# Four spectral products summed by accumulating stores from GpSimd's queue, and an inverse transform that loads the sums

## The chip, the cores and the metric

The kernel runs on one core of a Trainium2 chip. The metric is device time in microseconds (us) of one execution. A core has five engines with instruction streams of their own: PE (TensorE, matrix products), ACT (ScalarE), DVE (VectorE), POOL (GpSimd) and SP (SyncE, used here only to issue transfers). They meet through semaphores. Transfers (DMAs) run on 16 DMA engines that all queues share.

## The reference

Input x is (4, 56, 56, 128). Layer 0 is a neighbourhood-attention block (7x7 windows, 4 heads) with an MLP. Layer 1 works on the tokens t (4, 3136, 128): a linear attention that is added to t, and then the part that the change is in, a spectral filter (STU):

```python
def _stu_conv(phi, u, n):                      # n = 8192
    Vf = jnp.fft.rfft(phi, n=n, axis=0)        # 16 filters
    Uf_p = jnp.fft.rfft(u, n=n, axis=1)
    Uf_m = jnp.fft.rfft(u * sgn3, n=n, axis=1)
    U_plus  = jnp.fft.irfft(Vf[None, :, :, None] * Uf_p[:, :, None, :], n=n, axis=1)[:, :sl]
    U_minus = jnp.fft.irfft(Vf[None, :, :, None] * Uf_m[:, :, None, :], n=n, axis=1)[:, :sl]
    return U_plus, U_minus * sgn[None, :, None, None]
out = einsum('btkd,k,kde->bte', U_plus, s, Mpp) + einsum('btkd,k,kde->bte', U_minus, s, Mpm)
out = out + sum_i  shift(u, i) @ Mu[i]         # three taps
# four such sums over the first T/1, T/2, T/4, T/8 tokens, weighted by a straight-through gumbel choice
```

For each frequency the spectrum of the tokens (complex) is multiplied by a filter spectrum that has already absorbed the matrices (complex). One complex product needs four real ones: real = RR - II, imaginary = RI + IR.

## The kernel before, in words

The work runs in four parts. Front (0 to about 830 us) is layer 0, the linear attention and the preparation of the filter; Spectrum (about 735 to 875 us, beside the end of the front) is the forward transform of the tokens, stored to HBM as Ud. Neither is touched except for layout, names of semaphores and one constant.

Filters (875 to 1646 us) goes through 784 frequency slots in 28 chunks of 28 slots. `Filters.STAGES` is 56. A group P of four stages (4P to 4P+3) works on chunks 2P and 2P+1, and half the output features at a time: after stages 4P and 4P+1 the sums of the first 64 features are whole (store 2P), after stages 4P+2 and 4P+3 those of the others (store 2P+1). All engines follow one list of steps, written out in `order()` (L1326 to L1346), each in its own program order. Per stage there are 32 `filter` steps (PE makes a spectrum of the filter in a PSUM bank, L1374 and L1377; ACT copies the even ones to SBUF, L1415, and DVE the odd ones, L1429) and 28 `sums` steps (PE multiplies it with the tokens' spectrum, L1396). Filter products use four banks in turn, so product u waits until product u-4 has been copied (L1366, L1367); a `whole` one (i % 8 < 4) is issued as a pair and waits for two copies. In stage order, sums 7 to 13 follow filters 8 to 15 of the next stage, and then comes filter 16. The sums of an odd stage leave PSUM for the tile YS (L1421, ACT, after sums 7, 15, 23 and 27). SP stores YS to Yd in four transfers (L1493), all four real products of every frequency. In ACT's program the copy of YS after sums 7 stands ahead of its copies of filters 12 and 14.

GpSimd's program before holds only the `load` steps: `planes` (L1446 to L1474) rotates chunk c into one of three buffers U7. Chunk c takes the buffer of chunk c-3, so it waits (L1439) until PE has done the sums on that: chunk 2P+3 waits for half the sums of stage 4P+3 (14 of 28), chunk 2P+4 for all of them. In the list, `load 2P+3` stands at the head of stage 4P, `store 2P` behind stage 4P+1, `load 2P+4` at the head of stage 4P+3 and `store 2P+1` behind stage 4P+3. SP's `load` waits until the tile UL is free, which is when `planes` of the chunk before has ended (L1298).

Inverse (1646 to 1844 us) loads Yd (`load_y`, L1522), forms the two differences and sums on DVE (`combine`, L1648 to L1670, result YC), and PE does the inverse transform (L1596), 24 products for each of 16 steps t, plus a reversal (`turn`, L1603). DVE adds the parts into RN, which SP stores to the output.

Of the kernel before, what the change touches and what calls it, by code (L numbers as in the profile page):

```python
# [11 lines left out]
G = 98  # L12
# [222 lines left out]
class Front:  # L235
# [235 lines left out]
    def scalar(self, e):  # L471
        S, col = self.S, self.col
        for k, n in self.order:
# [21 lines left out]
            elif k == "q_keep":  # L495
# [10 lines left out]
                if i == 0 and b < 2:  # L506
                    e.wait_ge(S["kzero"], b + 1)
# [332 lines left out]
    def gpsimd(self, q):  # L840
        S, ch = self.S, self.pool_steps
        for k, n in self.order:
            if k == "setup" and n == 0:
# [8 lines left out]
                q.memset(self.kP[0][:, :, :], 0.0).then_inc(S["kzero"], 1)  # L852
# [5 lines left out]
            elif k == "setup" and n == 2:  # L858
                q.memset(self.kP[1][:, :, :], 0.0).then_inc(S["kzero"], 1)
# [20 lines left out]
            elif k == "z_clear":  # L880
                zero = self.kP[1].rearrange("p a b -> p (a b)")
                if n == 0:
                    q.wait_ge(S["kzero"], 2)
# [4 lines left out]
            elif k == "a_ones":  # L888
                q.wait_ge(S["csum"], NJ * n + NJ)
                if n:  # L890
                    q.wait_ge(S["kvmm"], n)
                q.tensor_scalar(self.kv[:, 1, :], self.ones, self.cs[n % 2][:, 128:129], None, ALU.mult).then_inc(S["kv1"], 1)
            elif k == "a_pre":
                q.wait_ge(S["xnc"], 2 * n + 2)
                q.wait_ge(S["kvw"], 2 * (n // NJ) + 2)
                q.tensor_tensor(self.rows(n), self.rows(n), self.kv[0:TB, 4:5, :].broadcast_to([TB, 4, 128]),
                                ALU.add).then_inc(S["addkv"], 1)
            elif k == "p_load":
                q.memset(self.sg, 1.0).then_inc(S["pset"], 1)
                for par in range(2):  # L900
                    q.dma_start(self.D["VbD"][par, :, KF:KT], self.D["c_ar"][par]).then_inc(S["d_ar"], 16)
# [28 lines left out]
    def setup(self, e, part):  # L930
# [15 lines left out]
        e.dma_start(self.ident[:, :], D["c_id"]).then_inc(S["d_first"], 16)  # L946
# [25 lines left out]
    def sync(self, e):  # L972
        S, D = self.S, self.D
        for k, n in self.order:
# [39 lines left out]
            elif k == "p_load":  # L1014
# [3 lines left out]
                e.wait_ge(S["pset"], 1)  # L1018
# [289 lines left out]
class Filters:  # L1308
# [44 lines left out]
    def tensor(self, e):  # L1353
        S = self.S
        for k, s, i in self.order():
# [24 lines left out]
            elif k == "sums":  # L1380
# [10 lines left out]
                if par == 0 and i % 8 == 0 and s >= 2:  # L1391
                    e.wait_ge(S["ys"], 4 * (s // 2 - 1) + bk + 1)
# [17 lines left out]
    def scalar(self, e):  # L1410
        S = self.S
        for k, s, i in self.order():
# [3 lines left out]
            elif k == "sums" and s % 2 and i in (7, 15, 23, 27):  # L1416
                bk, n = i // 8, 2 if i == 27 else 4
                e.wait_ge(S["sums"], 28 * s + i + 1)
                if s >= 2:
                    e.wait_ge(S["d_y"], 64 * (s // 2))  # L1420
                e.activation(self.YS[:, 4 * bk:4 * bk + n, :].rearrange("p g x -> p (g x)"),  # L1421
                             self.banks[:, 2048 + 512 * bk:2048 + 512 * bk + 128 * n], ACT.Copy).then_inc(S["ys"], 1)

    def vector(self, v):
        S = self.S
        for k, s, i in self.order():
            if k == "filter" and i % 2:
                dst, src = self.evict_filter(v, s, i)
                v.tensor_copy(dst, src).then_inc(S["gm_dve"], 1)  # L1429

    def gpsimd(self, q):
# [14 lines left out]
    def planes(self, q, c, u, u7, w, n):  # L1446

        S, ch = self.S, self.pool_steps
        a = u7.rearrange("d s (m r b) -> d s m r b", m=7, r=2)[:, :, 0:3]
# [3 lines left out]
        same, got = u7[:, :, 24:56].rearrange("d s (x b) -> d s x b", b=4), u.rearrange("d b s x -> d s x b")  # L1453
        if c < NCH // 2:
            q.tensor_copy(same, got)  # L1455
        else:
            src = same.rearrange("d s (m r) b -> d s m r b", r=2)
            q.tensor_tensor(same[:, 0:n:2], got[:, 0:n:2], got[:, 1:n:2], ALU.add)  # L1458
            ch.tick(q.tensor_tensor(same[:, 1:n:2], got[:, 0:n:2], got[:, 1:n:2], ALU.subtract))
            q.wait_ge(ch.sem, ch.n)  # L1460
            if c == NCH // 2:
                q.tensor_copy(same[:, 0], got[:, 0])
                ch.tick(q.tensor_scalar(same[:, 1], got[:, 1], -1.0, None, ALU.mult))
                q.wait_ge(ch.sem, ch.n)
# [10 lines left out]

    def sync(self, e):
        S, D = self.S, self.D
        for k, c, _ in self.order():
# [10 lines left out]
            elif k == "store":  # L1489
                e.wait_ge(S["ys"], 4 * c + 4)  # L1490
                P, half = c // 2, c % 2
                for x in range(4):
                    e.dma_start(D["Yd"][56 * P:56 * P + 56].rearrange("(g s) r h x -> s r g h x", s=4)[x, :, :, half, :],  # L1493
                                self.YS[32 * x:32 * x + 32, :, :]).then_inc(S["d_y"], 16)
            elif k == "inverse":
# [3 lines left out]
                elif c == 2:  # L1499
                    e.wait_ge(S["d_y"], 64 * (NCH // 2))  # L1500
                    for a in range(4):
                        load_y(e, D, D["YL0"], a, 0, 0).then_inc(S["d_ylh"], 16)
                else:
                    e.wait_ge(S["d_y"], 64 * (NCH - 2))
# [46 lines left out]
class Inverse:  # L1551
# [4 lines left out]
    def __init__(self, nc, ctx, D, S, chains):  # L1556
# [3 lines left out]
        yl1 = sb("YL1", [G, 8192])  # L1560
        D["YL1"] = [yl1[:, 0:4096], yl1[:, 4096:8192]]
        self.YL = [D["YL0"], D["YL1"]]
        self.YC = [sb("YC0", [G, 2, 8, 2, 128])]
        D["rev"] = sb("rev2", [G, G])[:, :]
        self.YC.append(sb("YC1", [G, 2, 8, 2, 128]))
# [20 lines left out]
    def sums(self, e, kind, t, a0, a1):  # L1586
# [19 lines left out]
    def tensor(self, e):  # L1606
        S = self.S
        e.wait_ge(S["d_iv"], 32)
        e.wait_ge(S["yc"], 1)
# [3 lines left out]
        e.wait_ge(S["yc"], 2)  # L1613
        e.wait_ge(S["ys"], 4 * NCH)
# [3 lines left out]
        e.wait_ge(S["yc"], 3)  # L1618
# [5 lines left out]
        for t in range(2, 16):  # L1624
            if t % 2 == 0:
                e.wait_ge(S["yc"], t + 2)
# [5 lines left out]
            if t % 2 == 0:  # L1632
                e.wait_ge(S["yc"], t + 3)
# [14 lines left out]
    def combine(self, v, n, h, k, a0=0, a1=4):  # L1648

        S = self.S  # L1650
        yl = self.YL[n % 2][h].rearrange("p (n r h k e) -> p n r h k e", n=8, r=2, h=2, k=2)[:, 2 * a0:2 * a1]
        yc = self.YC[n % 2].rearrange("p k a q (h e) -> p k (a q) h e", h=2)
        if k == 0 and a0 == 0:
            if n == 0:
                v.wait_ge(S["d_ylh" if h == 0 else "d_yl0"], 64 if h == 0 else 48)
                v.wait_ge(S["sums"], 28 * (Filters.STAGES - 1))
            elif h == 0:
                v.wait_ge(S[f"d_yl{n % 2}"], (48 if n % 2 == 0 else 128) + 128 * (n // 2))
                if n >= 2:
                    v.wait_ge(S["idft"], 8 * (n - 1))  # L1660
        if a0 == 3 and k == 0:
            v.wait_ge(S["d_ylh"], 80)
        hs, op = slice(8 * h + 2 * a0, 8 * h + 2 * a1), (ALU.subtract, ALU.add)[k]
        ins = v.tensor_tensor(yc[:, k, hs], yl[:, :, 0, :, k], yl[:, :, 1, :, 1 - k], op)
        if h == 0:
            self.steps.tick(ins)
            v.wait_ge(self.steps.sem, self.steps.n)
            ins = v.tensor_copy(yc[0:1, k, 0:2], yl[0:1, 0:2, k, :, k])  # L1668
        if k == 1:
            ins.then_inc(S["yc"], 1)  # L1670

    def vector(self, v):
        S, w, ch = self.S, self.D["wsel"], self.steps
        for k in range(2):
            self.combine(v, 0, 0, k)
        for k in range(2):
            self.combine(v, 0, 1, k, 0, 3)
        for k in range(2):
            self.combine(v, 0, 1, k, 3, 4)
        for t in range(17):  # L1680
# [15 lines left out]
            if t < 16:  # L1696
                rn = self.RN[n % 2]
                if q == 0 and 0 < n < 7:
                    for k in range(2):
                        self.combine(v, n + 1, 1, k)  # L1700
# [16 lines left out]
                if t == 0:  # L1717
                    for h in range(2):
                        for k in range(2):
                            self.combine(v, 1, h, k)  # L1720
                if q == 1 and n + 2 < 8:
                    for k in range(2):
                        self.combine(v, n + 2, 0, k)

    def sync(self, e):
        S, D = self.S, self.D
        for n in range(8):
            if n + 2 < 8:
                e.wait_ge(S["yc"], 2 * n + 3)
                for a in range(8):  # L1730
                    load_y(e, D, self.YL[n % 2], a, (n + 2) // 2, n % 2).then_inc(S[f"d_yl{n % 2}"], 16)
# [14 lines left out]
INVERSE_SIGNALS = "yc idft half gh rows tdif tmm turned kept d_rn0 d_rn1 d_o0 d_o1".split()  # L1746


def program(nc, x, ln1_w, ln1_b, w_qkv, b_qkv, rpb, w_proj, b_proj, ln2_w, ln2_b, w_fc1, b_fc1, w_fc2, b_fc2,
            Wq, bq, Wk, bk, Wv, bv, sigma, phi, M_u, M_pp, M_pm, log_w, gumbel,  # L1750
            c_id, c_fwd, c_vdft, c_tw, c_inv, c_ar, c_msk, c_rev, out):
    with ExitStack() as ctx:
# [12 lines left out]
                 Un=dr("Un", [NB, SLOTS, 512]), Ud=dr("Ud", [128, NB, SLOTS * 8]), Yd=dr("Yd", [SLOTS, 32, 2, 128]),  # L1765
# [4 lines left out]
                 YL0=[zone[0:G, 4096:8192], zone[0:G, 12288:16384]], banks=banks)  # L1770
# [31 lines left out]
def tables():  # L1802
# [42 lines left out]
    C2[392:, 196:] *= -1.0  # L1845
    inv = np.stack([C1, C2], 0).reshape(2, 8, 98, 392).transpose(2, 0, 1, 3)
# [4 lines left out]
def shape_constants():  # L1851
# [8 lines left out]
    return {"c_id": np.eye(128, dtype=np.float32), "c_fwd": fwd, "c_vdft": vdft, "c_tw": tw, "c_inv": inv,  # L1860
# [23 lines left out]
```

## Time and profile before

| | us |
|---|---|
| median of 3 runs (1840.15 to 1850.67) | 1843.27 |
| the profiled execution | 1845.46 |
| its span (first to last instruction) | 1844.1 |
| PE busy in the span | 1735.1 (94%) |
| DVE busy | 1314.0 (71%) |
| ACT busy | 1200.3 (65%) |
| POOL busy | 638.5 (35%) |

The profile covers one execution. A "busy" engine runs an instruction. A wait is put down to the instruction that came last. PEclk is the granted clock of TensorE as a share of full speed. The DMA share is that of the 16 DMA engines together. A queue named SPq or POOLq is the issuing side of a transfer; "to landing" is from the issue until the data are there.

### The profile page before, as it was taken

What the parts mean: (1) busy time and instruction counts of PE and PEld (TensorE: products, weight loads), DVE (VectorE), ACT (ScalarE), POOL (GpSimd) and SP (SyncE); (2) the same over time, 40 slices, a digit from 0 to 9 for tenths busy, and PEclk for the clock granted to TensorE, in tenths of its full rate; (3) what the DMA queues carried; (4) which work ended last, traced back from release to release, by engine and by line L of the source; (5) the groups of instructions that cost most, each with busy time, mean ns of one, the idle gap of its engine ahead of it and who ended that gap; (6) DMA issues with size and microseconds to landing.
All of it is one profiled execution on the core that took longest, in us unless ns stands there. A gap on an engine that the chain in (4) does not pass through costs nothing.

```text
span 1844.1 us, 76476 instructions
## 1 busy us (share of the span) xinstructions
PE 1735.1 (94%) x32475; PEld 1391.2 (75%) x32475; DVE 1314.0 (71%) x3787; ACT 1200.3 (65%) x2619; POOL 638.5 (35%) x815
## 2 busy tenths in 40 slices
PE   5899999999999998988899999999999999999998
PEld 3566666666767666888788888888888888876666
DVE  2677778888877766694677777777777777647666
ACT  5788888887877654556677777777777777640000
POOL 6555555655555533040533122333323233100000
PEclk8999999999999998989999999999999999999999
DMA  4422333433233313387322212222221222368772
GB/s 118 114 80 75 104 84 91 113 90 97 73 99 85 95 53 98 132 242 231 94 56 59 56 46 68 68 59 57 58 58 45 68 68 55 89 177 215 209 203 78
DMA packets 266001, 182.52 MB, mean 99 GB/s; under 512 B 39888, under 2 KB 263022, under 8 KB 263966
## 3 DMA queue, kind: packets, MB, share of 16 engines
q1 hardware_dynamic: 262782, 176.07, 35.2%
q8 instruction: 258, 4.23, 0.9%
q0 software_dynamic: 640, 1.16, 0.2%
q10 hardware_dynamic: 2240, 0.40, 0.1%
q14 instruction: 81, 0.66, 0.1%
HBM read 107.03 MB, written 70.63 MB: 96 GB/s over the span
## 4 chain that ended last, share of the span: by engine, by line
PE 66%; DVE 13%; issue 5%; DMA 5%; POOL 4%; ACT 4%; SPq 3%; DVEq 0%; POOLq 0%; ACTq 0%
PE banks L1396 20%; PE banks L1374 10%; PE banks L1377 9%; PE banks L406 5%; DVE zone L607 4%; PE banks L400 3%; PE banks L1596 3%; PE banks L365 2%; SPq L1524 2%; PE banks L355 2%; DMA YL<-Yd 2%; PE banks L413 2%; PE banks L379 2%; DVE st L594 1%; PE banks L453 1%
## 5 line engine op out<-in xcount | busy, mean ns | idle before, releaser
L1429 DVE COPY Gm<-banks 128x448 f32<-128x448 f32 x896 | 553.2, 639 | 214.2 <-PE banks L1374 127.4
L1415 ACT ACTIVATE Gm<-banks 128x448 f32<-128x448 f32 x896 | 515.6, 629 | 202.7 <-PE banks L1374 151.3
L1396 PE MATMUL banks<-Gm,U 128*32 128x128 f32 x12544 | 519.0, 275 | 15.0 <-issue 8.7
L1396 PEld LDWEIGHTS banks<-Gm,U 128*32 128x32 f32 x12544 | 340.4, 110 | 60.2 <-issue 54.7
L1377 PE MATMUL banks<-V,zone 118*32 118x224 bf16 x7040 | 294.3, 260 | 0.5 <-issue 0.4
L1374 PE MATMUL banks<-V,zone 118*128 118x224 bf16 x1824 | 215.3, 261 | 0.8 <-ACT qT L1203 0.5
L869 POOL TENSOR_TENSOR W<-W,mx 128x280 f32<-128x280 f32 x196 | 130.6, 666 | 227.4 <-DVE mx L656 226.0
L1377 PEld LDWEIGHTS banks<-V,zone 118*32 118x32 bf16 x7040 | 194.9, 96 | 1.8 <-issue 1.4
L1374 PEld LDWEIGHTS banks<-V,zone 118*128 118x128 bf16 x1824 | 157.1, 98 | 47.3 <-issue 39.2
L1596 PE MATMUL banks<-YC,zone 98*98 98x256 f32 x768 | 171.3, 383 | 3.3 <-DVE YC L1668 3.3
L1596 PEld LDWEIGHTS banks<-YC,zone 98*98 98x98 f32 x768 | 128.1, 167 | 50.3 <-issue 7.6
L519 ACT ACTIVATE W<-W,mx 128x140 f32<-128x140 f32 x392 | 156.7, 404 | 0.3
L607 DVE TENSOR_SCALAR zone<-XR,zone 112x128 f32<-112x128 f32 x336 | 152.1, 498 | 4.6 <-POOL zone L831 3.2
L365 PE MATMUL banks<-ident,W 128*98 128x128 f32 x784 | 123.3, 281 | 24.4 <-ACT W L529 15.2
L649 DVE CUSTOM_DVE_ANT_0 W<-banks,zone 128x140 f32<-128x140 f32 x392 | 102.6, 298 | 54.3 <-PE banks L355 27.0
L365 PEld LDWEIGHTS banks<-ident,W 128*98 128x98 f32 x784 | 87.0, 130 | 62.9 <-POOL W L869 36.5
L529 ACT ACTIVATE W<-banks 98x512 f32<-98x512 f32 x196 | 115.1, 587 | 28.4 <-PE banks L365 27.8
L831 POOL TENSOR_TENSOR zone<-zone 112x4 f32<-112x4 f32 x112 | 119.6, 1068 | 9.3
L1646 ACT ACTIVATE PB<-banks 98x512 f32<-98x512 f32 x16 | 9.6, 598 | 173.1 <-PE banks L1596 173.1
L1455 POOL COPY U<-UL 128x896 f32<-128x896 f32 (+2 forms) x14 | 24.2, 1730 | 276.6 <-PE banks L1396 205.8
L594 DVE BATCH_NORM_STATS2 st<-XR 112x6 f32<-112x128 f32 x448 | 107.4, 281 | 8.4 <-DMA XR<-in_x_dram 5.8
L1458 POOL TENSOR_TENSOR U<-UL 128x448 f32<-128x448 f32 x14 | 25.3, 1805 | 252.9 <-PE banks L1396 232.1
(174 smaller groups left out, 2684.8 us busy)
## 6 DMA issues: line engine op xcount, KB each, us to landing
Yd<-YS SPq DMA_DIRECT2D x112, 224.0 KB, 4.3
W<-Vd SPq DMA_DIRECT2D x392, 49.0 KB
zone<-Yd SPq DMA_DIRECT2D x32, 392.0 KB
YL<-Yd SPq DMA_DIRECT2D x32, 392.0 KB
UL<-Ud SPq DMA_DIRECT2D x27, 448.0 KB, 4.0
zone<-Mbf SPq DMA_DIRECT2D x28, 256.0 KB
Vd<-W SPq DMA_DIRECT2D x56, 112.0 KB
T<-XR SPq DMA_DIRECT2D x28, 224.0 KB, 2.6
```

What stands on the lines that cost most here:

```text
L365: ins = e.transpose(self.psum[4][0:G, 256 * c + 128 * j:256 * c + 128 * j + 128], self.PN[n % 3][:, j, G * c:G * c + G], self.ident[:, :])
L519: ins = e.activation(self.PB[n % 3][:, j, :], self.SB[n % 3][:, j, :], ACT.Exp, bias=self.mx[n % 4][:, j:j + 1], scale=-1.0, accum_out=sel ...
L594: ins = v.bn_stats(self.st[:, m, :], self.row(g)[:, 128 * m:128 * m + 128])
L607: ins = v.tensor_scalar(x[:, m, 0:128], self.row(g)[:, 128 * m:128 * m + 128], self.mv[k][g % 2][:, m, 0:1], self.rs[k][g % 2][:, m:m + 1] ...
L831: ins = q.tensor_tensor(rs, rs, self.half[0:TB, :], ALU.pow)
L869: q.tensor_tensor(self.inner(self.PN[n % 3]), self.PB[n % 3], r, ALU.mult).then_inc(S["pn"], 1)
L1374: ins = e.matmul(pt[:, q, :], M, V, start=True, stop=True)
L1377: ins = e.matmul(pt[32 * x:32 * x + 32, q, :], M[:, 32 * x:32 * x + 32], V, start=True, stop=True, tile_position=(0, 32 * x))
L1396: ins = e.matmul(p[32 * x:32 * x + 32, :], self.U7[(2 * P + ch) % 3][:, sl, 8 * (3 - q):8 * (3 - q) + 32], self.Gm[:, par, r:r + 2, :], st ...
L1415: e.activation(dst, src, ACT.Copy).then_inc(S["gm_act"], 1)
L1429: v.tensor_copy(dst, src).then_inc(S["gm_dve"], 1)
L1596: ins = e.matmul(p[:, 256 * c:256 * c + 256], self.D["IV"][c][:, a, x:x + G], self.YC[n % 2][:, int(k), a], start=a == lo and (c == 0 or n ...
```

## The change

- The columns of U7 are ordered so that each group of two neighbouring rows of the sums is the product with the real part (even partition) and the imaginary part (odd partition) of the tokens' spectrum.
- YS is evicted by ACT after sums 7 and 23 and by DVE after sums 15 and 27, each in two instructions; the second multiplies the columns of the filter's imaginary part by +1 on even and -1 on odd partitions. These evictions wait (from stage 3 on) for d_ya, the accumulating transfers of the chunks before, where they waited for the stores d_y.
- A store is one transfer of the 64 even partitions (two transfers and two small ones for the first two chunks). Then GpSimd adds the odd partitions to the same rows with two accumulating transfers (`accum_op=ALU.add`, real and imaginary columns crossed). Its new step `add_up` is taken at the place of `store` in the list.
- Yd holds half as much, `load_y` moves half, three tiles YL are in turn, PE reads them without `combine`, which is gone. The loads for group n=2 are issued ahead of the first `load_out`.
- The constant of the first row of the inverse table changes sign, and some semaphores are merged.

The core of the diff:

```diff
+            elif k == "sums" and s % 2 and i in (7, 23):
+                dst, src = self.evict_sums(e, s, i)
+                e.activation(dst[:, :, 0:64], src[:, :, 0:64], ACT.Copy)
+                e.activation(dst[:, :, 64:128], src[:, :, 64:128], ACT.Copy, scale=self.D["wsel"][:, 16:17]).then_inc(S["ys_act"], 1)
+    def evict_sums(self, e, s, i):
+        S, bk, n = self.S, i // 8, 2 if i == 27 else 4
+        e.wait_ge(S["sums"], 28 * s + i + 1)
+        if s >= 2:
+            e.wait_ge(S["d_ya"], added(s // 2))
 ...
     def gpsimd(self, q):
         S, D = self.S, self.D
         for k, c, _ in self.order():
+            if k == "store":
+                self.add_up(q, c)
             if k != "load":
                 continue
 ...
+    def product_rows(self, c):
+        P, half = c // 2, c % 2
+        rows = self.D["Yd"][896 * P:896 * P + 896, half].rearrange("(g i) x -> i g x", i=64)
+        return [(rows[16:64], 32, 128, 0), (rows[0:16, 1:14], 0, 32, 1)] if P == 0 else [(rows, 0, 128, 0)]
+    def add_up(self, q, c):
+        S = self.S
+        q.wait_ge(S["d_y"], stored(c + 1))
+        for rows, p0, p1, g0 in self.product_rows(c):
+            for k in range(2):
+                q.dma_start(rows[:, :, 64 - 64 * k:128 - 64 * k], self.YS[p0 + 1:p1:2, g0:14, 64 * k:64 * k + 64],
+                            accum_op=ALU.add).then_inc(S["d_ya"], 16)
 ...
             elif k == "store":
-                e.wait_ge(S["ys"], 4 * c + 4)
-                for x in range(4):
-                    e.dma_start(D["Yd"][56 * P:56 * P + 56].rearrange("(g s) r h x -> s r g h x", s=4)[x, :, :, half, :],
-                                self.YS[32 * x:32 * x + 32, :, :]).then_inc(S["d_y"], 16)
+                e.wait_ge(S["ys_act"], 2 * c + 2)
+                e.wait_ge(S["ys_dve"], 2 * c + 2)
+                for rows, p0, p1, g0 in self.product_rows(c):
+                    e.dma_start(rows, self.YS[p0:p1:2, g0:14]).then_inc(S["d_y"], 16)
 ...
         e.wait_ge(S["d_ylh"], 64)
-        e.wait_ge(S["d_y"], 64 * NCH)
+        e.wait_ge(S["d_ya"], added(NCH))
         load_y(e, D, D["YL0"], 7, 0, 0).then_inc(S["d_ylh"], 16)
         load_y(e, D, D["YL1"], 7, 0, 1).then_inc(S["d_yl1"], 16)
         e.wait_ge(S["sums"], 28 * Filters.STAGES)
+        for a in range(8):
+            load_y(e, D, D["YL2"], a, 1, 0).then_inc(S["d_yl2"], 16)
         load_out(e, D, S, 0)
```

## Rows read from the trace of the kernel before

**Rows 1.** Windows (us; busy PE, PEld, DVE, ACT, POOL; PEclk; DMA share; GB/s), Filters.

```profile
1000.00:1100.00 100.00, 99.24 (x2863) 87.22 (x2864) 73.40 (x120) 73.34 (x133) 23.56 (x22) 1.00 0.26 63
```

**Rows 2.** Waits in Filters, 890 to 1645 us: total, times, longest.

```profile
POOL U L1458 <- PE banks L1396: 232.1, 9, 33.1
POOL U L1455 <- PE banks L1396: 205.8, 7, 34.7
```

**Rows 3.** Timeline of POOL (start, us, ...): first and last instruction of `planes`, chunks 3, 4, 17.

```profile
938.88 1.86 POOL L1455 COPY U<-UL 128x896 f32<-128x896 f32 x1 [32.40 <-PE banks L1396]
945.65 1.09 POOL L1474 TENSOR_TENSOR U<-U,UL 128x336 f32<-128x336 f32 x1
950.70 1.86 POOL L1455 COPY U<-UL 128x896 f32<-128x896 f32 x1 [3.95 <-DMA UL<-Ud]
...
1314.55 1.84 POOL L1458 TENSOR_TENSOR U<-UL 128x448 f32<-128x448 f32 x1 [31.86 <-PE banks L1396]
1322.38 1.10 POOL L1474 TENSOR_TENSOR U<-U,UL 128x336 f32<-128x336 f32 x1
```

**Rows 4.** Timeline of ACT: evictions of YS in stage 3 and the first of stage 5.

```profile
936.71 0.60 ACT L1421 ACTIVATE YS<-banks 128x512 f32<-128x512 f32 x1
...
945.43 0.38 ACT L1421 ACTIVATE YS<-banks 128x256 f32<-128x256 f32 x1
963.81 0.60 ACT L1421 ACTIVATE YS<-banks 128x512 f32<-128x512 f32 x1
```

**Rows 5.** Timeline, all engines, about filter 16 of the list in stage 3.

```profile
937.20 1.11 ACT L1415 ACTIVATE Gm<-banks 128x448 f32<-128x448 f32 x2
937.89 0.84 PE L1396 MATMUL banks<-Gm,U 128*32 128x128 f32 x24
938.66 0.94 PE L1374 MATMUL banks<-V,zone 118*128 118x224 bf16 x8
```

**Rows 6.** Groups by line: total busy, mean ns of one.

```profile
L1415 ACT ACTIVATE Gm<-banks 128x448 f32<-128x448 f32 x896 | 515.6, 629 | 202.7 <-PE banks L1374 151.3 <-PE banks L1377 49.4 <-DMA Ud<-qT 1.7
L1462 POOL COPY U<-UL 128x32 f32<-128x32 f32 x1 | 0.2, 233 | 0.1
```

**Rows 7.** GpSimd's transfers of before: durations (ns, min/median/max) of L919; KB each, us to landing.

```profile
L919 POOL DMA_DIRECT2D Vd<-kP x6: 533/548/778, 39.1 to 52.8; - x6
Vd<-kP POOLq DMA_DIRECT2D x6, 93.0 KB, 2.9
```

**Rows 8.** Stores of YS by SP: KB each, us to landing, and windows around the first.

```profile
Yd<-YS SPq DMA_DIRECT2D x112, 224.0 KB, 4.3
918.00:922.00 4.00, 4.00 (x110) 3.44 (x111) 2.96 (x5) 2.97 (x7) 0.00 (x0) 1.00 0.60 138
922.00:926.00 4.00, 4.00 (x132) 3.62 (x128) 3.13 (x6) 2.75 (x6) 0.00 (x0) 1.00 0.53 110
```

**Rows 9.** PE's timeline around an idle stretch of the Spectrum part, and two windows.

```profile
787.01 2.82 PE L1188 MATMUL banks<-XR,W 98*128 98x196 f32 x16
813.58 5.60 PE L1182 MATMUL banks<-XR 98*128 98x196 f32 x16 [6.14 <-DVE XR L1242]
816.00:820.00 4.00, 4.00 (x13) 3.69 (x13) 3.93 (x13) 1.68 (x2) 1.26 (x2) 0.51 1.07 414
820.00:824.00 4.00, 4.00 (x25) 3.75 (x24) 3.83 (x16) 0.97 (x2) 1.26 (x2) 1.00 0.60 179
```

**Rows 10.** Timeline at the start of Inverse: last eviction, store, load of the last piece, PE.

```profile
1645.88 20.96 PE L1596 MATMUL banks<-YC,zone 98*98 98x256 f32 x96
1646.45 5.84 SPq L1493 DMA_DIRECT2D Yd<-YS  x4
1660.49 0.76 DVE L1664 TENSOR_TENSOR YC<-zone 98x256 f32<-98x256 f32 x2 [14.81 <-DMA zone<-Yd]
1671.04 6.45 PE L1596 MATMUL banks<-YC,zone 98*98 98x256 f32 x16 [3.26 <-DVE YC L1668]
```

**Rows 11.** Waits of PE in Inverse, 1645 to 1844 us.

```profile
PE banks L1603 <- DVE DF L1708: 7.3, 6, 1.7
```

More of the change, by code:

```diff
@@ L1415, in scalar @@
                 e.activation(dst, src, ACT.Copy).then_inc(S["gm_act"], 1)
[L1416 to L1422, printed above, removed]
+            elif k == "sums" and s % 2 and i in (7, 23):
[7 more added lines that the diff above has]
+            e.wait_ge(S["d_ya"], added(s // 2))
+        src = self.banks[:, 2048 + 512 * bk:2048 + 512 * bk + 128 * n].rearrange("p (g x) -> p g x", x=128)
+        return self.YS[:, 4 * bk:4 * bk + n], src
     def vector(self, v):
         S = self.S
+        v.wait_ge(S["d_sign"], 16)
         for k, s, i in self.order():
@@ L1429, in vector @@
                 v.tensor_copy(dst, src).then_inc(S["gm_dve"], 1)
+            elif k == "sums" and s % 2 and i in (15, 27):
+                dst, src = self.evict_sums(v, s, i)
+                v.tensor_copy(dst[:, :, 0:64], src[:, :, 0:64])
+                v.tensor_scalar(dst[:, :, 64:128], src[:, :, 64:128], self.D["wsel"][:, 16:17], None, ALU.mult
+                                ).then_inc(S["ys_dve"], 1)
     def gpsimd(self, q):
@@ L1448, in planes @@
         S, ch = self.S, self.pool_steps
-        a = u7.rearrange("d s (m r b) -> d s m r b", m=7, r=2)[:, :, 0:3]
+        a, x7 = (u7.rearrange("d s (m b r) -> d s m r b", m=7, r=2)[:, :, i:j] for i, j in ((0, 3), (3, 7)))
         s4 = u.rearrange("d b s (m r) -> d s m r b", m=4, r=2)
@@ L1452, in planes @@
         src, spare = s4, s4[:, :, 1:4, 0]
[L1453 to L1459, printed above, removed]
-            q.wait_ge(ch.sem, ch.n)
[L1461 to L1464, printed above, removed]
+        for r in range(2):
+            to, of = x7[:, :, :, r], s4[:, :, :, r]
+            if c < NCH // 2:
+                q.tensor_copy(to, of)
+            else:
+                src = x7
+                q.tensor_tensor(to[:, 0:n:2], of[:, 0:n:2], of[:, 1:n:2], ALU.add)
+                ch.tick(q.tensor_tensor(to[:, 1:n:2], of[:, 0:n:2], of[:, 1:n:2], ALU.subtract))
+        if c >= NCH // 2:
+            q.wait_ge(ch.sem, ch.n)
+        if c == NCH // 2:
+            for r in range(2):
+                q.tensor_copy(x7[:, 0, :, r], s4[:, 0, :, r])
+                ch.tick(q.tensor_scalar(x7[:, 1, :, r], s4[:, 1, :, r], -1.0, None, ALU.mult))
+            q.wait_ge(ch.sem, ch.n)
         R, I, re, im = src[:, :, 1:4, 0], src[:, :, 1:4, 1], a[:, :, :, 0], a[:, :, :, 1]
@@ L1489, in sync @@
             elif k == "store":
-                e.wait_ge(S["ys"], 4 * c + 4)
-                P, half = c // 2, c % 2
-                for x in range(4):
-                    e.dma_start(D["Yd"][56 * P:56 * P + 56].rearrange("(g s) r h x -> s r g h x", s=4)[x, :, :, half, :],
-                                self.YS[32 * x:32 * x + 32, :, :]).then_inc(S["d_y"], 16)
+                e.wait_ge(S["ys_act"], 2 * c + 2)
+                e.wait_ge(S["ys_dve"], 2 * c + 2)
+                for rows, p0, p1, g0 in self.product_rows(c):
+                    e.dma_start(rows, self.YS[p0:p1:2, g0:14]).then_inc(S["d_y"], 16)
+                if c < 2:
+                    for k in range(2):
+                        e.dma_start(D["Yd"][0:16, c, 64 * k:64 * k + 64], self.YS[k:32:2, 0, 64 * k:64 * k + 64]
+                                    ).then_inc(S["d_y"], 16)
             elif k == "inverse":
@@ L1499, in sync @@
                 elif c == 2:
-                    e.wait_ge(S["d_y"], 64 * (NCH // 2))
+                    e.wait_ge(S["d_ya"], added(NCH // 2))
                     for a in range(4):
@@ L1503, in sync @@
                 else:
-                    e.wait_ge(S["d_y"], 64 * (NCH - 2))
+                    e.wait_ge(S["d_ya"], added(NCH - 2))
                     for a in range(4, 7):
@@ L1559, in __init__ @@
         self.psum = D["psum"]
[L1560 to L1563, printed above, removed]
+        for i in (1, 2):
+            yl = sb(f"YL{i}", [G, 4096])
+            D[f"YL{i}"] = [yl[:, 0:2048], yl[:, 2048:4096]]
+        self.YL = [D["YL0"], D["YL1"], D["YL2"]]
         D["rev"] = sb("rev2", [G, G])[:, :]
-        self.YC.append(sb("YC1", [G, 2, 8, 2, 128]))
         self.RN = D["RN"] = [sb(f"RN{i}", [G, 2, 4, 256]) for i in range(2)]
@@ L1646, in scalar @@
             e.activation(self.PB[t % 2][:, :], self.bank("two", t), ACT.Copy).then_inc(S["half"], 1)
[L1648 to L1670, printed above, removed]
     def vector(self, v):
         S, w, ch = self.S, self.D["wsel"], self.steps
[L1674 to L1679, printed above, removed]
         for t in range(17):
@@ L1697, in vector @@
                 rn = self.RN[n % 2]
-                if q == 0 and 0 < n < 7:
-                    for k in range(2):
-                        self.combine(v, n + 1, 1, k)
                 v.wait_ge(S["idft"], INVERSE_DONE["odd", t])
@@ L1716, in vector @@
                                            ).then_inc(S["kept"], 1)
[L1717 to L1723, printed above, removed]
     def sync(self, e):
@@ L1743, in sync @@
         e.wait_ge(S["d_o1"], 32 * 3 + 96)
-INVERSE_SIGNALS = "yc idft half gh rows tdif tmm turned kept d_rn0 d_rn1 d_o0 d_o1".split()
+INVERSE_SIGNALS = "idft half gh rows tdif tmm turned kept d_rn0 d_rn1 d_o0 d_o1".split()
 def program(nc, x, ln1_w, ln1_b, w_qkv, b_qkv, rpb, w_proj, b_proj, ln2_w, ln2_b, w_fc1, b_fc1, w_fc2, b_fc2,
```

64 lines of the change are left out of this document (36 added, 28 removed).

## The prediction

> **What bounds the kernel now.** I read the page's busy shares first, then the windows over Filters, then the waits, and last the timelines of POOL, ACT and PE about one group of four stages. PE is busy 99 of 100 us in Filters, at full clock [rows 1]. The reader is to see there that neither ACT nor DVE (73 of 100 each) nor the DMA engines (0.26) is near a bound, so that work taken from them in this part buys nothing, while anything that stops PE costs its full length. The waits show that POOL spends most of Filters waiting for PE: 232 and 206 us in 16 waits of up to 35 us [rows 2]. These waits look like free room. They are the point of the case, since POOL's program is in order: what stands behind such a wait waits too. In Inverse PE is busy too, with two kinds of gaps: 3.3 us before the second group [rows 10] and 7.3 us in six waits for DVE [rows 11].
>
> **Where the new transfers stand in POOL's program.** The list gives POOL: `planes` of 2P+3, `add_up` of 2P, `planes` of 2P+4, `add_up` of 2P+1. `planes` of 2P+3 has to wait until PE has done half the sums of stage 4P+3; for chunk 3 it started at 938.88, after 32.4 us of waiting [rows 3]. `add_up(2P)` could go two stages earlier, but it is behind that wait. In the same stage 4P+3 ACT meets the eviction after sums 7, at 936.71 [rows 4], and from now on that one waits for d_ya of chunk 2P. So ACT stops there, 2.2 us before POOL even starts `planes`. Behind it in ACT's program are its copies of filters 12 and 14 (the pair at 937.20) [rows 5]. PE still does up to sums 13 (the group at 937.89), which is what POOL waits for, and then comes to filter 16 (938.66) [rows 5], which needs the bank of filter 12. PE stops. There is no deadlock, since sums 13 stand before filter 16, but nothing covers the stop: it lasts from POOL's start until the eviction and one copy of ACT are done. This happens for P = 0 to 12, 13 times (the last group has no `planes` left).
>
> **The length of one stop.** Four terms.
> - `planes`: 938.88 to 946.74 is 7.9 us for a chunk under 14 (six of the stops), 1314.55 to 1323.48 is 8.9 us from 14 on (seven) [rows 3]. Together 47 + 62 = 110 us. The new layout adds one instruction for the first kind and two for the second; elements are the same, a small copy costs 0.233 us [rows 6], so 13 times 0.2 to 0.4 us, 4 us. Sum 114 us.
> - The two accumulating transfers, from POOL's first issue to both landed; I call it T. No row shows an accumulation. Each moves 64 x 14 runs of 256 B, 896 runs, 224 KB. The stores of before move 1792 runs of 512 B in two windows of 4 us with shares 0.60 and 0.53 [rows 8]: 4.5 us of all 16 engines, 40 ns for a run. The two transfers have 1792 runs as well. If a run costs the same, 4.5 us; if it goes by bytes, 2.3 us; if the target's old value must be read as a further run, 9 us. Ahead is one issue, 0.55 us, and behind the last run some 2.1 us (a 93 KB transfer of POOL lands 2.9 us after its issue of 0.55, with 0.2 us of runs) [rows 7]. So T is 4.9, 7.1 or 11.6 us. Above that, if the issue goes in proportion to runs, 548 ns for 93 runs [rows 7] make 5.3 us for 896, and T = 10.6 + 4.5 + 2.1 = 17.2 us. I take 10.5 us, near 11.6, since an addition must read both operands, and since the UL load (448 KB, issued when `planes` ends) runs beside it. 13 x 10.5 = 137 us.
> - Restart: two half evictions of ACT instead of one of 0.6 us [rows 4], say 0.4 each, then one copy of 0.63 us [rows 6] and a hand-over of 0.2: 1.6 us, 13 times 21 us.
> - Clock: after 6.1 us without work PE did 16 products in 5.60 us that took 2.82 at full clock, and the window 816 to 820 has PEclk 0.51, the lower level (1.2 GHz), the next one 1.00 again [rows 9]. So about 3 us for a stop, 39 us. Below nothing is excluded, as the granted clock was never above 1.00.
>
> Sum 311 us in Filters. Speaking for less, by a rule of the Trainium skill ("DMA: Bandwidth & Descriptors", Anatomy of one DMA): a transfer issued by GpSimd takes 2.0 us and its bytes at 436 GB/s, 2.5 us for 224 KB; an estimate by that page for two in a row is T = 5 us and a total 71 us lower. The same page warns of runs under 512 B, whose writes read first; here they are 256 B. Our stores have none below 512 B, so no row weighs the one against the other.
>
> **The second half of a group.** `add_up(2P+1)` follows `planes` of 2P+4, which after the change finds its load long landed and starts at the end E of stage 4P+3 (about 945.4 [rows 4]; before, it waited 3.95 us for UL until 950.70 [rows 3]). The next eviction, in stage 5, came at 963.81, E + 18.4, and PE would stop 2.2 us later less 1.4 for the eviction and a copy: E + 19.2. `planes` takes 8.0 or 9.2 of it, so T up to 11.2 (first six) or 10.0 us (the others) is hidden. At 10.5: 7 x 0.5, 4 us. The store itself (issue about E + 1, landing 4.3 [rows 8]) is done before `planes` ends. SP's order is as before; its store 2P+1 comes when `planes` of 2P+3 has ended, now earlier than E.
>
> **Evictions on DVE, PE's products.** Two of four evictions go to DVE, which has 27% idle; PE does the same products. Nothing at either end.
>
> **Inverse.** Gone is `combine`, which PE waited for at the second group, 3.3 us [rows 10] and again about 3 of clock; and of the six waits for DVE five, 7.3 - 1.6 = 5.7 us [rows 11], because `combine` stood before the addition that they wait for. Loads are halved. Put in their place: the last chunk is added before its piece can be loaded: eviction ended about 1646.5, store + 4.3, T without the UL load 9, load and landing 3.7 (as 1656.8 to 1660.5): 1663.5. PE needs it after 80 of the first 96 records, 1645.9 + 17.5 = 1663.4 [rows 10]. Just in time; at the bounds of T, 4 us early or 8 late. SP then issues 8 loads of the third tile (about 0.9 us each) ahead of `load_out(0)`, which lands about 1672 and before was needed at 1667; that holds DVE 5 us and PE perhaps 3, and again 3 of clock. So + 6 against - 6 and - 5.7: I take - 5 us, between - 12 and + 8.
>
> The forecast is 1845.5 + 311 + 4 - 5 = 2155 us for an execution like the profiled one, which lay 2.2 above the median: **2153 us**.
>
> **Rivals.**
> - Short transfers: a run goes by bytes, T = 4.9. Then 13 x 5.6 = 73 us less, no second-half term (4): 2076 us. For it: DMA engines are idle three quarters of Filters. Against: runs of 256 B are half the size of any that the stores use.
> - Slow issue or slow addition: T = 17.2. Then 13 x 6.7 = 87 us more, and the second half shows: 6 x 6.0 + 7 x 7.2 = 86 us in place of 4, + 8 in Inverse: 2153 + 87 + 82 + 13 = 2335 us. For it: no instruction of POOL in the trace has so many runs. Against: 0.53 to 0.78 us for each of the few there are. A rule of the Trainium skill goes the same way ("SBUF — State Buffer", A bandwidth-pool intuition that's wrong): a DVE copy in a two-port mode keeps GpSimd from writing descriptors; an estimate by that page's 620 against 3100 ns is 2.5 us more for each issue, 65 us in all. DVE is mostly stopped with PE in the stop, so I give it no row.
> - On the other side, no stop: POOL has issued `add_up(2P)` before it waits for PE. Then T has from the end of stage 4P+1 to the next eviction, over 20 us, all is hidden, and only Inverse counts: 1843 - 5 = 1838 us. It decides at whether the step stands before or behind `planes` of 2P+3 in POOL's program. The list says behind.
> - The change does what it says (half of Yd's bytes, no `combine`), but those bytes were not on the path: the time of this rival is that of the others.
>
> **How the numbers follow.** Forecast (T between 7 and 13.5) 0.56, short 0.16, slow 0.24, no stop 0.04. Each microsecond of T is 13 us, beyond 10 to 11 it is 26. The range is 2065 to 2320: it leaves out the last case, the lower part of short and the upper part of slow, together 2 in 10. About 0.5% is what a measurement of this kernel can tell from no change. The time of no stop (1838) lies within 0.5% of the median: same 0.03, faster 0.01, slower 0.96.
>
> **What would show it.** In the profile of the changed kernel: PE at about 80% or less; ACT's eviction after sums 7 of stages 3, 7, 11 and on waiting for a transfer into Yd some 20 us; PE idle 13 times for some 18 to 22 us, starting with POOL's `planes`; PEclk below 1.00 after each; PE's work between stops unchanged. The first issue of `add_up` to the release of ACT gives T. Wrong would be: stops at every store (then T is over 11), or none; PE at full clock after a stop (39 us less); `planes` longer than 9.5 us.

## The result, and the profile after

| | before | after |
|---|---|---|
| median, us | 1846.4 (4 runs, 1840.2 to 1850.7) | 2095.8 (4 runs, 2092.4 to 2099.5) |
| ratio to before | | 1.134 (95%: 1.131 to 1.137) |
| span of the profiled execution | 1844.1 | 2092.7 |
| PE busy | 1735.1 (94%) | 1759.9 (84%) |
| Inverse, from its first product to the end of the span | 198.2 | 193.9 |

The change costs 249 us, 13% of the time, though `combine` is gone from DVE and 13 MB of HBM reads are gone too (107.0 MB before, 94.2 after). The first view is the waits of the changed kernel from 880 us on (who waited for whom, total, times, longest):

```profile
ACT YS L1418 <- DMA Yd<-YS: 241.6, 15, 21.3
PE banks L1374 <- ACT Gm L1415: 229.5, 15, 20.6
PE banks L1374 <- DVE Gm L1436: 8.1, 1, 8.1
```

ACT's eviction of the sums (L1418) waited 15 times for the additions, 241.6 us in all, and PE's first filter product after it waited for ACT as often, 229.5 us. Before, PE had no such wait in Filters. The next view is the timeline of the stop in stage 7; POOL's rows, then SP's and ACT's, then PE's:

```profile
1008.79 1.87 POOL L1470 COPY U<-UL 128x448 f32<-128x448 f32 x2 [34.24 <-issue]
...
1015.24 1.24 POOL L1491 TENSOR_TENSOR U<-U,UL 128x336 f32<-128x336 f32 x1
1016.41 2.79 POOL L1505 DMA_DIRECT2D Yd<-YS  x2
1016.50 0.55 SPq L1299 DMA_DIRECT2D UL<-Ud  x1
1023.83 0.39 ACT L1418 ACTIVATE YS<-banks 128x256 f32<-128x256 f32 x1 [17.08 <-DMA Yd<-YS]
1007.80 0.84 PE L1396 MATMUL banks<-Gm,U 128*32 128x128 f32 x24
1025.07 1.67 PE L1374 MATMUL banks<-V,zone 118*128 118x224 bf16 x8 [16.43 <-ACT Gm L1415]
```

Read it by the starts. PE ends its 14th sums at 1008.6; POOL, which waited for them, starts `planes` at 1008.79 and needs 7.6 us; only then does it issue the two additions (1016.41). They have landed when ACT goes on at 1023.83, 7.4 us later, and PE starts its next products 1.24 us after that. 7.6 + 7.4 + 1.2 is the idle time of 16.43 us but for the hand-over. The same row appears 13 times, for P = 0 to 12, with 16.1 to 20.7 us, 227 us in all. The windows about the first stop (PE ran again from 952.54) show the clock; the last three numbers of a row are PEclk, DMA share and GB/s:

```profile
949.00:952.00 3.00, 0.00 (x0) 0.00 (x0) 0.00 (x0) 0.70 (x3) 0.00 (x0) 0.50 0.94 82
954.00:956.00 2.00, 2.00 (x42) 1.71 (x44) 1.46 (x4) 0.80 (x2) 0.00 (x0) 0.50 0.00 0
958.00:960.00 2.00, 2.00 (x39) 1.44 (x33) 0.88 (x3) 0.83 (x2) 0.00 (x0) 0.83 0.00 0
960.00:964.00 4.00, 4.00 (x132) 3.62 (x127) 3.53 (x7) 3.37 (x8) 1.69 (x2) 1.00 0.01 4
```

PEclk is 0.50, the lower level, in the stop and for about 6 us after it, then 1.00; the eight products that took 0.94 us [rows 5] took 1.67. The budget of the span's 248.6 us: Filters, from PE's first product in it to the first of Inverse, grew from 770.9 to 1027.1 us, by 256.3. In it 227.2 us are idle in the 13 stops, and PE's busy time for the same products went from 754.6 to 782.5 us, 27.9 more or 2.1 for a stop, which is the clock. Another 1.9 us is a wait in stage 29. Inverse gave back 4.3 us. Filters also began 3.4 us earlier in this execution (871.6 against 875.0; in x2 and x5 below it began at 876.6 and 876.1, so this is not put down to the change).

The transfers after, from the page (packets, MB, share of the DMA engines; then transfers, KB each, us to landing), beside [rows 8]:

```profile
q0 software_dynamic: 51712, 14.00, 7.3%
Yd<-YS SPq DMA_DIRECT2D x26, 448.0 KB, 3.9
Yd<-YS POOLq DMA_DIRECT2D x52, 224.0 KB, 5.8
```

### The profile page after: what moved, and what is told of

Read it like the earlier page. It is cut to its first block, busy times and chain, and to the rows that moved or that the text cites. A ratio compares the mean times of both kernels' runs of the same rounds, so it can differ in the third digit from the quotient of the medians.

```text
span 2092.7 us, 76579 instructions
## 1 busy us (share of the span) xinstructions
PE 1759.9 (84%) x32475; PEld 1410.3 (67%) x32475; DVE 1302.9 (62%) x3849; ACT 1183.8 (57%) x2619; POOL 720.2 (34%) x920
## 3 DMA queue, kind: packets, MB, share of 16 engines
q0 software_dynamic: 51712, 14.00, 7.3%
## 4 chain that ended last, share of the span: by engine, by line
issue 25%; PE 12%; POOL 10%; DMA 7%; DVE 0%; ACT 0%; SPq 0%; POOLq 0%; ACTq 0%; DVEq 0%
PE banks L1644 7%; DMA UL<-Ud 4%; PE banks L1396 2%; DMA Yd<-YS 2%; POOL U L1491 1%; POOL U L1473 1%; POOL U L1474 1%; PE banks L1374 1%; POOL UL L1486 1%; POOL U L1489 1%; PE banks L1377 1%; POOL U L1483 1%; POOL U L1484 1%; POOL U L1470 1%; POOL U L1487 1%
## 5 line engine op out<-in xcount | busy, mean ns | idle before, releaser
L1396 PE MATMUL banks<-Gm,U 128*32 128x128 f32 x12544 | 528.9, 280 | 6.3 <-issue 5.5
L1374 PE MATMUL banks<-V,zone 118*128 118x224 bf16 x1824 | 226.4, 270 | 238.1 <-ACT Gm L1415 229.5
L1396 PEld LDWEIGHTS banks<-Gm,U 128*32 128x32 f32 x12544 | 346.6, 112 | 52.7 <-issue 50.7
L1374 PEld LDWEIGHTS banks<-V,zone 118*128 118x128 bf16 x1824 | 163.1, 101 | 289.1 <-ACT Gm L1415 235.7
L1377 PE MATMUL banks<-V,zone 118*32 118x224 bf16 x7040 | 301.4, 266 | 0.2 <-issue 0.2
L1418 ACT ACTIVATE YS<-banks 128x256 f32<-128x256 f32 x56 | 21.3, 380 | 247.4 <-DMA Yd<-YS 241.6
L1473 POOL TENSOR_TENSOR U<-UL 128x224 f32<-128x224 f32 x28 | 27.1, 967 | 343.9 <-issue 296.8
L1470 POOL COPY U<-UL 128x448 f32<-128x448 f32 (+2 forms) x28 | 25.3, 933 | 336.7 <-issue 224.1
L529 ACT ACTIVATE W<-banks 98x512 f32<-98x512 f32 x196 | 114.9, 586 | 28.3 <-PE banks L365 27.9
L1505 POOL DMA_DIRECT2D Yd<-YS x60 | 80.6, 1621 | 82.6 <-DMA Yd<-YS 59.4
L1644 PE MATMUL banks<-YL,zone 98*98 98x256 f32 x480 | 107.2, 383 | 0.0
```

What stands on the lines that cost most here:

```text
L529: e.activation(self.PT[n % 3], self.psum[4][0:G, :], ACT.Copy).then_inc(S["keep"], 1)
L1374: ins = e.matmul(pt[:, q, :], M, V, start=True, stop=True)
L1377: ins = e.matmul(pt[32 * x:32 * x + 32, q, :], M[:, 32 * x:32 * x + 32], V, start=True, stop=True, tile_position=(0, 32 * x))
L1396: ins = e.matmul(p[32 * x:32 * x + 32, :], self.U7[(2 * P + ch) % 3][:, sl, 8 * (3 - q):8 * (3 - q) + 32], self.Gm[:, par, r:r + 2, :], st ...
```

## The experiments

The theory: what stops PE is that in GpSimd's program the additions of chunk 2P stand behind `planes` of 2P+3, which waits for PE. The main rival: the accumulating transfers are dear by themselves, wherever they stand. Ratios are to runs of the kernel before on the same chip, whose median there lay between 1848.8 and 1849.9 us.

**The additions of even chunks ahead of `planes`** (x1_even_adds_early). In GpSimd's program alone:

```diff
+        steps = [(k, c) for k, c, _ in self.order() if k in ("load", "store")]
+        for j in range(len(steps) - 1):
+            if steps[j][0] == "load" and steps[j][1] % 2 and steps[j + 1] == ("store", steps[j][1] - 3):
+                steps[j], steps[j + 1] = steps[j + 1], steps[j]
```

> The changed kernel, but GpSimd issues the additions of chunk 2P ahead of planes(2P+3); those of chunk 2P+1 stay behind planes(2P+4). Theory A (the 13 stops come from the place of the additions in GpSimd's program): the stops of 16 to 21 us at stages 4P+3 go. But planes(2P+4) then waits again for the load of UL, as before the change, so the additions of 2P+1 start 13.3 us (later chunks 15.4) after the end E of stage 4P+3 and land T = 7.4 us later: E + 20.7 to E + 22.8 against the E + 19.2 that PE needs. So stops of 1.5 to 3.6 us in stages 4P+5, with or without a dip of the clock: 1865 to 1910 us. Rival B (the accumulating transfers cost by themselves, by their load on the DMA engines or on GpSimd): the stops at stages 4P+3 shorten by no more than planes (8 to 9 us each), time over 1960 us.

Measured 1910.9 us, ratio 1.032 (1.028 to 1.035), 1 us above the upper end of the theory's span (1910) and far under the rival's 1960. The long stops are gone; the short ones that the theory names stand in their place. PE's timeline, chunks of the first and of the second half:

```profile
1028.46 1.00 PE L1374 MATMUL banks<-V,zone 118*128 118x224 bf16 x8 [3.05 <-ACT Gm L1415]
...
1454.42 1.67 PE L1374 MATMUL banks<-V,zone 118*128 118x224 bf16 x8 [5.09 <-ACT Gm L1415]
```

2.7 to 3.7 us for the first chunks and 3.6 to 7.9 for the later ones, where I had 1.5 and 3.6 (the 7.9 is the stop in which GpSimd paused 4.8 us between the two issues). The place was right, the length about 1.5 us too short.

**All additions ahead of `planes`** (x2_all_adds_early). The same without `steps[j][1] % 2`, so that chunks 2P+1 move too.

> As the one before, and the additions of 2P+1 ahead of planes(2P+4) too. Theory A: they start when their store has landed, about E + 6, and have landed at E + 14, so no stop in Filters is left; what remains of the change is Inverse (4.3 us shorter in the changed kernel): 1838 to 1846 us, ratio 0.994 to 1.000. Rival B: still over 1960 us. Rival C (delays of 4 to 5 us between the two additions, which four of the 13 stops show, are a full ring of descriptors): they show here too and cost nothing.

Measured 1843.2 us, ratio 0.996 (0.995 to 0.998): the kernel with every accumulating transfer in it is as fast as the one before or 0.4% faster. No wait of PE for an eviction is left in Filters (of its waits only the 8.3 us at the head, see x9, is over 2.1 us), and its page has the same transfers; their larger share is of a shorter span (160 us of it against 153):

```profile
q0 software_dynamic: 51712, 14.00, 8.7%
```

So off the path the load of the additions on the DMA engines and on GpSimd costs nothing that can be seen; the rival falls. What rival C names is here too. The timeline of POOL for chunk 4: the second addition starts 3.37 us after the end of the first, and the profile names nothing that it waited for:

```profile
1034.08 1.41 POOL L1509 DMA_DIRECT2D Yd<-YS  x1 [14.24 <-DMA Yd<-YS]
1038.85 1.37 POOL L1509 DMA_DIRECT2D Yd<-YS  x1 [3.37 <-issue]
```

It now ends before anyone needs it.

**The loads of RN0 ahead of those of the third tile** (x3_all_early_rn_first), on top of it:

```diff
+        load_out(e, D, S, 0)
         for a in range(8):
             load_y(e, D, D["YL2"], a, 1, 0).then_inc(S["d_yl2"], 16)
-        load_out(e, D, S, 0)
```

> As the one before, and the two loads of RN0 ahead of the eight loads of the third tile YL. In the changed kernel DVE waited 5.2 us for RN0 and PE then 6.05 us for DVE, and after it the clock was low for one more group (11.98 against 10.52 us). Theory: this wait goes, 6 to 8 us less than the one before: 1831 to 1839 us, ratio 0.991 to 0.996. Rival: PE then waits for the third tile instead, 0 to 3 us less.

Measured 1835.2 us, ratio 0.992 (0.989 to 0.994). Beside x2 the rows of PE's second `turn`, first x2, then x3:

```profile
1681.92 2.00 PE L1655 MATMUL banks<-DF,rev 98*98 98x512 f32 x2 [7.11 <-DVE DF L1727]
```

```profile
1672.22 1.07 PE L1655 MATMUL banks<-DF,rev 98*98 98x512 f32 x2 [0.90 <-DVE DF L1727]
```

The wait of 7.1 us is 0.9, and the product itself takes 1.07 in place of 2.00: PEclk stays 1.00 about it in x3 (1667 to 1676), where it is 0.55 in x2 (1681 to 1686). The time is 8.0 us less than that of x2. Inverse is 186.7 us long, 11.5 less than before the change (198.2) and 7.6 less than in x2 (194.3).

**The wait without the additions** (x4_before_with_wait). To the kernel before, one wait in ACT's program, at the eviction of the sums:

```diff
+                if s % 4 == 3 and i == 7 and s < 52:
+                    e.wait_ge(S["u7"], 2 * (s // 4) + 5)
```

> The kernel before the change with one wait added and nothing else: ACT's eviction after sums 7 of stages 3, 7, ... 51 waits until planes(2P+3) has ended. There are no accumulating transfers. Theory A: PE stops 13 times for planes (7.9 or 8.9 us) and some 1.2 us of restart, and the clock takes 2 to 3 us more each time: 13 x 11.5 to 12.5 = 150 to 165 us, time 1993 to 2011 us. Rival B: nearly the time of before, as ACT has a quarter of its time free.

Measured 2000.4 us in a single run, within the theory's 1993 to 2011. PE's stops in it are the same in each half, six and seven times:

```profile
947.21 1.67 PE L1374 MATMUL banks<-V,zone 118*128 118x224 bf16 x8 [8.86 <-ACT Gm L1415]
...
1337.06 1.68 PE L1374 MATMUL banks<-V,zone 118*128 118x224 bf16 x8 [9.94 <-ACT Gm L1415]
```

6 x 8.86 + 7 x 9.94 = 122.7 us; its span is 155.0 above that of before, so 32.3 us or 2.5 us for a stop come on top, the clock for the most part (PE is busy 27.1 us longer, 1762.2 against 1735.1). So three fifths of the loss (155.0 of 248.6) are there without a single accumulating transfer: it is enough that ACT's eviction waits until `planes` has ended.

**What T consists of.** Three kernels with the stops left in and one thing about the transfers changed. The first overwrites (x5_plain_not_added): `accum_op=ALU.add` is taken out.

> The changed kernel, but GpSimd's transfers overwrite and do not add (same bytes, runs, waits and place; the sums are therefore not formed and the output is not the reference's). Theory D (an addition costs a further read of each run): T, 7.4 us from first issue to ACT's release in the changed kernel, becomes 5.5 to 6.5 us, and the time falls by 13 times as much: 2070 to 2085 us. Rival E (GpSimd's two issues of 1.4 us and the way of the last data set T): T 7 us or more, 2088 to 2100 us.

The second issues one of the two additions (x6_one_addition): `for k in range(1)`, and `added` counts half.

> The changed kernel with only the first of the two accumulating transfers of each chunk (half of the additions is left out, so the output is not the reference's). Theory: T loses one issue of 1.4 us and one share of the movement, to 4.5 to 5.5 us, and no stop has the delay of 3 to 5 us between two issues: 2096 - 13 x 2.4 - 4 x 3 = 2050 to 2060 us. Rival C (a ring of descriptors fills after so many transfers): the delay is still there, now ahead of some chunk's transfer. Rival F: T is fixed cost only, and stays 7 us: 2080 us or more.

The third issues one of whole rows (x8_one_of_512B): `q.dma_start(rows, self.YS[p0 + 1:p1:2, g0:14], accum_op=ALU.add)`.

> The changed kernel with one accumulating transfer for each chunk, of whole rows (896 runs of 512 B in place of 2 x 896 of 256 B; the real and imaginary columns are not crossed, so the output is not the reference's). If runs set the movement, T is as with one transfer of 256 B (4.5 to 5.5 us) and the time within 8 us of that kernel; if bytes do, T is about a microsecond longer and the time 10 to 20 us above it.

T is from POOL's first issue to ACT's row. The pairs of rows are the stop in stage 7 in x5, x6 and x8; the table has the median of T over the 13 stops of each:

```profile
1019.10 1.64 POOL L1505 DMA_DIRECT2D Yd<-YS  x2
1024.68 0.39 ACT L1418 ACTIVATE YS<-banks 128x256 f32<-128x256 f32 x1 [15.24 <-DMA Yd<-YS]
```

```profile
1018.44 1.40 POOL L1505 DMA_DIRECT2D Yd<-YS  x1
1024.19 0.38 ACT L1418 ACTIVATE YS<-banks 128x256 f32<-128x256 f32 x1 [15.41 <-DMA Yd<-YS]
```

```profile
1017.11 1.40 POOL L1505 DMA_DIRECT2D Yd<-YS  x1
1023.94 0.38 ACT L1418 ACTIVATE YS<-banks 128x256 f32<-128x256 f32 x1 [16.47 <-DMA Yd<-YS]
```

| | T, us (lowest to highest) | ratio to before (95%) | median, us |
|---|---|---|---|
| changed kernel, 2 additions of 256 B runs | 7.10 (6.08 to 10.58) | 1.134 (1.131 to 1.137) | 2095.8 |
| x5, 2 plain transfers of 256 B runs | 5.52 (4.32 to 8.41) | 1.115 (1.112 to 1.118) | 2061.0 |
| x6, 1 addition of 256 B runs | 5.64 (4.40 to 5.80) | 1.113 (1.109 to 1.116) | 2056.1 |
| x8, 1 addition of 512 B runs | 6.85 (5.94 to 7.14) | 1.123 (1.120 to 1.126) | 2075.7 |

The 7.4 us of stage 7, from which the expectations were worked out, is the longest T of the changed kernel without a pause of GpSimd between its two issues; ten stops have 6.1 to 7.4, and three with a pause of 4.3 to 4.7 us have 10.2 to 10.6. The addition itself costs 1.6 us of T, within what theory D said (rival E falls); the time fell further than its 2070 us, to 2061, as three of the five pauses went with it, two of them in stops. Leaving one addition out takes 1.5 us from T (I had 1.9 to 2.9), and no pause shows; here `planes` stands between any two transfers, which would hide one. The time is in the span I gave. Runs of twice the bytes cost 1.2 us more and 19.6 us in all, so bytes count, not the number of runs alone.

The lowest T of all four kernels is that of the last stop, and it is the only one in which SP issues no UL load beside the transfers. The rows of the changed kernel in stage 43 and in the last stop, stage 51:

```profile
1679.75 2.77 POOL L1505 DMA_DIRECT2D Yd<-YS  x2
1679.83 0.54 SPq L1299 DMA_DIRECT2D UL<-Ud  x1
1686.87 0.38 ACT L1418 ACTIVATE YS<-banks 128x256 f32<-128x256 f32 x1 [18.01 <-DMA Yd<-YS]
...
1832.13 2.77 POOL L1505 DMA_DIRECT2D Yd<-YS  x2
1838.21 0.38 ACT L1418 ACTIVATE YS<-banks 128x256 f32<-128x256 f32 x1 [16.95 <-DMA Yd<-YS]
```

T is 7.1 us with the load and 6.1 without; the median and the last stop are 5.5 and 4.3 in x5, 5.6 and 4.4 in x6, 6.9 and 5.9 in x8. So the UL load beside them holds the transfers up by some 0.9 to 1.2 us, by one stop in each of four kernels; no run takes it away by itself. Even so 4.3 us are left for the smallest, and only moving it off the path took those away.

**The wait for the signs** (x9_sign_wait_late, beside x3b_again_beside, which is x3 once more). In the changed kernel DVE waits at the head of Filters for the column of signs, which SP issues late: 15.8 us for DVE and 8.1 for PE (the third row of the first fence above). x9, on top of x3, waits at the first eviction instead:

```diff
-        v.wait_ge(S["d_sign"], 16)
 ...
         if s >= 2:
             e.wait_ge(S["d_ya"], added(s // 2))
+        else:
+            e.wait_ge(S["d_sign"], 16)
```

> As x3_all_early_rn_first, and the wait for the column of signs stands before the first eviction of the sums on ACT and on DVE, not at the head of DVE's program of Filters. In the changed kernel and in x3 DVE waited 15.8 us for that load and PE 8 us for DVE after its first filters; sums began at 892.8 us in x3, at 885.9 before the change. But before the change PE then waited 1.5 + 2.6 + 1.6 us for GpSimd's planes, so part of what goes comes back: 1 to 4 us less than x3, 1831 to 1834 us if x3 is 1835, ratio to before about 0.990. Rival: 6 to 8 us less.

> The kernel of x3_all_early_rn_first once more, on the chip and in the rounds of x9, to tell a difference of 2 us: ratio 0.990 to 0.993.

x9 took 1830.8 us, ratio 0.989 (0.988 to 0.991), x3 again 1836.0 us, 0.992 (0.990 to 0.993). That is 5.2 us less, a little more than my 1 to 4 and less than the rival's 6 to 8; the two intervals overlap, but the four times of each do not (1829.2 to 1832.7 and 1833.8 to 1837.5): the direction is clear, the size less so. In x9's waits PE has, in place of the 8.0 us for DVE, those for GpSimd that stood there before the change:

```profile
PE banks L1396 <- POOL U L1496: 5.3, 3, 2.7
```

x9 is the best version: 1.1% faster than the kernel before, where the change as made is 13% slower. Not tried: a second tile YS, which by the same argument would also take the wait off the path; it needs another 7168 B in each partition (14 x 128 values of 4 B).

## Why the prediction was right, point by point

**The bound and the place.** Right. The stop is where the prediction put it, 13 times, starts with `planes` of 2P+3, ends with an eviction and one copy, and goes when the additions stand ahead (x1, x2). x4 shows the same from the other side. Of the signs that were named, ACT's wait of some 20 us was 16.7 to 21.3, and PE's idle time of 18 to 22 us was 16.1 to 20.7; PE at 80% or less was 84%, as the stops were shorter than forecast.

**The size.** The forecast for the span was 310 us more, the trace has 248.6. Term by term, over the 13 stops:

| term | forecast, us | measured, us | from |
|---|---|---|---|
| `planes` | 114 | 107.5 | 7.6 (six) and 8.8 (seven), to the first issue |
| T | 137 (10.5 each) | 101.4 (7.8 on average) | 6.1 to 7.4 in ten stops, 10.2 to 10.6 in three |
| restart | 21 | 18.3 | 1.24 each and the hand-overs: 227.2 less the two rows above |
| clock | 39 | 27.9 | PE's busy time in Filters, 754.6 to 782.5 |
| second half of a group | 4 | 1.9 | one wait, in stage 29 |
| Inverse | - 5 | - 4.3 | 193.9 against 198.2 |
| not forecast | 0 | - 4.1 | 3.4 of it the earlier start of Filters |

The term that was most mis-sized is T, 36 of the 61 us. All terms of Filters were put too high, so no two errors there hid each other; the forecast of 2153 us lies 57 above the measured time. Of the three readings of a run's cost I took the dearest, 9 us of movement for a read of both operands, and added for the UL load. An addition does cost more than a plain transfer, but 1.6 us for the two and not 4.5. The UL load, issued 0.09 us behind, does cost, about 1 us. The value in the middle, 7.1, was the right one as a sum, in part by luck: it had 0.55 us ahead, 4.5 of movement and 2.1 behind, without a UL load. In the last stop, which has none, the DMA share is 0.00 until 1834, 1.9 us after the first issue, 1.00 to 1.78 from 1834 to 1838, and ACT goes on at 1838.21. On the issue, the low bound of 0.55 us was too low and the proportional 5.3 too high: 1.39 each.

**The second half of a group.** Its threshold (T of 10 to 11.2) was right: it shows only where a pause stretches T. The eviction of stage 29 went on at 1424.00, 11.3 us after the first addition of that chunk at 1412.74, and PE stopped for 1.9 us.

**Inverse.** The sum was right, and so were its terms but for one wait, which was twice as long as I had it: the waits for `combine` went, and the loads of RN0 behind eight others held DVE 5.2 us (I had 5) and PE 6.05 (I had 3), with a product of 2.00 in place of 1.07 us and 48 of 11.98 in place of 10.52 behind it (I had 3, it is 2.4).

**The rival of no stop** (1838 us) was priced too low for the step it named. With only `add_up(2P)` moved, x1 is at 1911: `planes` of 2P+4 then waits for its load again, and the additions of 2P+1 behind it come late. It takes both moves, and then it is 1843 us.

**Missed.** The wait of DVE for the signs at the head of Filters. I had counted "nothing at either end" for the evictions on DVE. In the changed kernel it cost little in sight, as part of it stood in place of the waits for GpSimd (x9: about 5 us).

**The price by the page.** By the page "DMA: Bandwidth & Descriptors" of the Trainium skill (Anatomy of one DMA) a transfer from GpSimd of 224 KB takes 2.5 us, an estimate from 2.0 us and the bytes at 436 GB/s. Here a plain one took 4.7 us from issue to landing in the median (x5) and an accumulating one 5.8 in the changed kernel and 5.2 in x2. For runs of 256 B the page's sum is about half of what the trace shows, and the measurement decides. As to the rule of the Trainium skill's page "SBUF — State Buffer" (A bandwidth-pool intuition that's wrong), by which a DVE copy can hold up GpSimd's descriptors, an issue took 1.39 us in the stop, with DVE idle, and 1.37 to 1.41 in x2, where DVE goes on copying from PSUM: no run here shows a lengthening.

## What to carry to other kernels

A transfer that an in-order engine issues inherits every wait that stands ahead of it in that engine's program; before giving an engine a new step, write down its program and ask when each wait ends, and who waits for what is behind it. An engine that is idle 65% of the time because it waits for the bottleneck is no free engine for a step that the bottleneck waits for. When such a step is needed, put it ahead of the long wait: here the place of `add_up` in GpSimd's program was worth 14% of the time (ratio 1.134 against 0.996).

## What the runs showed of the hardware that I had not expected

- An accumulating transfer from GpSimd makes far more packets than a plain one of the same bytes: 51712 packets for 14.00 MB in the changed kernel; in x5, with the same bytes and runs, the row of the queue is this:

```profile
q0 software_dynamic: 5184, 14.00, 2.1%
```

  640 packets are there in the kernel before too. The rest of the 51712 is one for each run (50112 runs of 256 B) and 16 for each of the 60 transfers; the rest of the 5184 is one for each partition of a transfer (3584) and 16 for each. x6 and x8, with half as many runs, have 26176 each, whether the run is 256 or 512 B. This is worked out from the access patterns in the kernels; all four counts fit it exactly.

- With the addition the issue of 896 runs takes 1.39 us of POOL against 0.80 to 0.82 for a plain one (two in 1.64 us); 93 runs took 0.55 [rows 7].
- Between the two additions of a chunk GpSimd sometimes pauses for 3.1 to 5.4 us, and the profile names no releaser. It comes at the same places in the changed kernel, x1, x2 and x3, whose times differ: between transfers 13 and 14, 21 and 22, 31 and 32, 49 and 50, 55 and 56 of the queue's 60. Plain transfers (x5) have it at the second and the fifth place only. It goes by the count of transfers and not by time, as far as these kernels show. What GpSimd does in the pause stays open; that a ring of descriptors is full then, as rival C had it, is not shown.
